# Three unmasked attentions of a decoder: scores also made with the keys on the partitions, row maxima added by TensorE

## What is computed

```python
        Q = (x @ Wq.T).reshape(B, xN, NUM_HEADS, HEAD_DIM)
        KV = (z @ Wkv.T).reshape(B, zN, 2, NUM_HEADS, HEAD_DIM)
        K = KV[:, :, 0]
        V = KV[:, :, 1]
        attn = jnp.einsum('bqhd,bkhd->bhqk', Q, K) * SCALE
        attn = jax.nn.softmax(attn, axis=-1)
        O = jnp.einsum('bhqk,bkhd->bqhd', attn, V).reshape(B, xN, DIM)
        return O @ Wo.T
```

## Time and profile before

| what | value |
|---|---|
| median of 3 runs | 4947.15 us |
| runs | 4947.15, 4937.4, 4949.03 us |
| span of the profiled execution | 4969.4 us, its own execution, 0.4% above that median |
| PE busy | 4410.3 us (89%) |
| DVE busy | 2640.3 us (53%) |
| ACT busy | 2593.2 us (52%) |
| POOL busy | 836.2 us (17%) |

### The profile page before, as it was taken

The page is one execution under the profiler, slowest core; times in us unless marked ns, Lnnn a source line. Parts: engine busy times, 40 slices in busy tenths (PEclk is TensorE's granted clock), DMA queues, the critical chain, the costliest instruction groups (busy, mean ns, idle before and its releaser), DMA issues.

```text
span 4969.4 us, 84778 instructions
## 1 busy us (share of the span) xinstructions
PE 4410.3 (89%) x29077; PEld 2535.4 (51%) x29077; DVE 2640.3 (53%) x6880; ACT 2593.2 (52%) x9813; POOL 836.2 (17%) x1454
## 2 busy tenths in 40 slices
PE   7888989989999999989799888998889888898796
PEld 3544764444454454448355444454455454554493
DVE  5555225655655655645454656556664565546523
ACT  4556434454454454453555556555655566555542
POOL 0111420011011011035021021110131021210350
PEclk9999989999999999999899989999999999999897
DMA  5000540000000000007000000000000000000172
GB/s 198 11 11 11 172 128 18 12 7 28 12 7 28 12 7 18 6 22 222 22 22 10 5 5 24 14 10 1 6 23 14 9 6 10 10 1 1 46 230 76
DMA packets 107750, 183.05 MB, mean 37 GB/s; under 512 B 13344, under 2 KB 69408, under 8 KB 107200
## 3 DMA queue, kind: packets, MB, share of 16 engines
q1 hardware_dynamic: 92544, 147.48, 9.9%
q0 software_dynamic: 13632, 28.04, 1.6%
q10 hardware_dynamic: 1152, 2.10, 0.1%
HBM read 126.33 MB, written 51.23 MB: 36 GB/s over the span
## 4 chain that ended last, share of the span: by engine, by line
PE 65%; DVE 20%; ACT 7%; issue 5%; DMA 2%; POOL 1%; SPq 0%; DVEq 0%; POOLq 0%; ACTq 0%
PE bank L713 8%; PE bank L866 7%; PE bank L883 6%; DVE rowmax L1693 6%; PE bank L745 4%; PE bank L1041 3%; PE bank L733 3%; PE bank L1152 3%; PE bank L1141 3%; PE bank L1023 3%; PE bank L790 3%; DVE probsT L1759 2%; PE bank L922 2%; PE bank L852 2%; ACT work L1323 2%
## 5 line engine op out<-in xcount | busy, mean ns | idle before, releaser
L1323 ACT ACTIVATE work<-bank,rowmax 128x128 f32<-128x128 f32 (+1 forms) x3072 | 1061.1, 398 | 208.6 <-DVE rowmax L1693 208.6
L1693 DVE TENSOR_REDUCE rowmax<-bank 128x4 f32<-128x512 f32 (+2 forms) x1152 | 614.0, 578 | 433.4 <-PE bank L866 314.8
L713 PE MATMUL bank<-mask_causal,identb 128*128 128x512 bf16 x2839 | 803.1, 394 | 22.6 <-DVE qd L1628 8.7
L883 PE MATMUL bank<-ident,work 128*128 128x128 f32 (+1 forms) x4096 | 641.0, 282 | 155.6 <-DVE probsT L1759 116.7
L1323 ACT ACTIVATION_READ_ACCUMULATOR work<-bank,rowmax 128x1 f32 x3072 | 753.1, 245 | 0.0
L883 PEld LDWEIGHTS bank<-ident,work 128*128 128x128 f32 (+1 forms) x4096 | 481.8, 144 | 377.7 <-DVE probsT L1759 196.8
L1759 DVE COPY probsT<-bank 128x512 f32<-128x512 f32 (+2 forms) x832 | 482.0, 601 | 55.3 <-PE bank L883 53.9
L713 PEld LDWEIGHTS bank<-mask_causal,identb 128*128 128x128 bf16 x2839 | 273.5, 101 | 290.7 <-issue 115.5
L866 PE MATMUL bank<-km,q 32*128 32x512 f32 (+2 forms) x1792 | 403.7, 562 | 1.9 <-issue 1.9
L2206 POOL TENSOR_TENSOR qd<-work 128x256 f32<-128x256 f32 (+1 forms) x64 | 64.7, 1012 | 1902.9 <-ACT work L1321 1836.5
L1257 ACT ACTIVATE part<-bank,eps 128x512 f32<-128x512 f32 x232 | 157.7, 680 | 383.8 <-PE bank L745 383.3
(11 more groups left out here) (336 smaller groups left out, 6902.5 us busy)
## 6 DMA issues: line engine op xcount, KB each, us to landing
slot<-in_w_L_ffn SPq DMA_DIRECT2D x78, 578.0 KB
slot<-in_w_stream SPq DMA_DIRECT2D x41, 512.0 KB
expert_rows<-slot SPq DMA_DIRECT2D x36, 516.0 KB, 6.3
slot<-in_w_L_ffn SPq DMA_DIRECT2D x39, 450.0 KB
qd<-expert_rows SPq DMA_DIRECT2D x117, 129.0 KB
back<-pair_rows SPq DMA_DIRECT2D x24, 512.0 KB, 5.3
slot<-in_w_stream SPq DMA_DIRECT2D x16, 256.0 KB
pair_rows<-qd,dest POOLq DMA_INDIRECT x234
```

The lines of the kernel that those rows point to most:

```text
L713: nc.tensor.matmul(b[:], identb[:], mask["causal"][:].unsqueeze(1).to_broadcast([P, 4, P]), start=True, stop=True)
L883: ins = nc.tensor.transpose(b[0:nk, j * P:(j + 1) * P], probs[t % 2][:, r, j, 0:nk], ident[:])
L1323: ins = nc.scalar.activation(out, raw, ACT.Exp, bias=top, accum_out=expsum[t % 2][:, 4 * r + j:4 * r + j + 1])
L1693: V.tensor_reduce(m[:, 4 * r:4 * r + J], banks.where(("scores", n, c, s, r))[:, 0:J * nk] .rearrange("p (j k) -> p j k", j=J), AX_X, ALU.m ...
```

## The change

The three attentions go through a new keyed_mha() on PE, ACT and DVE. For each item:

- PE makes the scores as before (L1026), from which only the maxima are taken, and makes them a second time with the keys on the partitions and the queries along the columns (L1037, 16 matmuls of 32 rows, 4 to a bank).
- DVE takes the 16 negated maxima, and splits each into a bf16 part and a bf16 rest in a tile `tops` (L1909, L1910). PE turns `tops` (L1045), ACT copies it to `topsT` (L1478), and PE adds it into the keyed banks by bf16 matmuls with a constant of ones and zeros, top_pick (L1056, 16 an item).
- ACT makes the exponential of a whole keyed bank in one instruction, straight to `probsT` (L1487, 4 an item). There are no transposes of probabilities and no copies of them.
- PE sums over the keys by matmuls with constant ones (L1075, 16 an item, in the attend form); ACT inverts the sums by a logarithm and an exponential (L1502, L1505). DVE's reciprocal and spread, PE's turn of the spread, ACT's copy of it and POOL's sums are gone.
- attend (L1094) and context (L1934) are as before but for the bank rings and the wait on `inverse` where it was on `wide_taken`. Output (L1106) takes its bank from the ring "second".
- The banks are two rings of three: "first" (0 to 2) for scores and turned maxima, "second" (3 to 5) for the keyed banks. Filler stands only ahead of items 0 and 1.

A round of PE is cut in two halves: scores of strips 0 and 1 of item t are interleaved with keyed matmuls of strips 2 and 3 of item t-1, and the other way round. Beside it: the constant average64 is gone (one scale in L1257's place), `after_mask` is bf16, `tops` is cleared once at the start. A part of keyed_mha() serves attentions with a mask or with a second use of the probabilities (`mask`, `post`); none of the three has these. The core of the diff:

```diff
+KEYED = ("L1_xattn", "L3_ffn", "L2_a2",)
+FRONT_ROWS, BACK_ROWS = (0, 1), (2, 3)
...
-                             "head": (4, 5)})
+                             "head": (4, 5), "first": (0, 1, 2), "second": (3, 4, 5)})
...
-            return not st["linear"] and not st["mask"] and r in POOL_SUMS
+            return not st["linear"] and not st["mask"] and not keyed(st) and r in POOL_SUMS
...
+                    if keyed(st):
+                        keyed_mha(st, second, then)
+                        return
...
+                def keyed_mha(st, second, then):
...
+                    def half(t, rows):
+                        back = BACK_ROWS if rows == FRONT_ROWS else FRONT_ROWS
+                        if t < GROUP:
+                            c, s = items[t]
...
+                            for r in rows:
+                                b = bank(("scores", n, c, s, r), ("row_max", (n, c, s, r)), "first")
...
+                        if 1 <= t <= GROUP:
+                            c, s = items[t - 1]
+                            for r in back:
+                                b = bank(("keyed", n, c, s, r), ("probsT", (n, c, s, r)), "second")
...
+                        for j in range(4):
+                            if t < GROUP:
+                                c, s = items[t]
+                                for r in rows:
+                                    g32 = slice(32 * r, 32 * r + 32)
+                                    b = banks.where(("scores", n, c, s, r))
+                                    if D == 32:
+                                        ins = nc.tensor.matmul(b[:, j * nk:(j + 1) * nk], q4[c][g32, j, s * P:(s + 1) * P],
+                                                               k4[c][g32, j, s * nk:(s + 1) * nk], start=True, stop=True)
+                                        if j == 3:
+                                            ins.then_inc(*made("scores", (n, c, s, r)))
+                                    elif j == 0:
+                                        nc.tensor.matmul(b[:, 0:4 * nk], B["q"][c][g32, s * P:(s + 1) * P],
+                                                         km[c][g32, s, :, 0:nk], start=not st["mask"], stop=True
+                                                         ).then_inc(*made("scores", (n, c, s, r)))
+                            if 1 <= t <= GROUP:
+                                c, s = items[t - 1]
+                                for r in back:
+                                    g32 = slice(32 * r, 32 * r + 32)
+                                    if D == 32:
+                                        keys, queries = k4[c][g32, j, s * nk:(s + 1) * nk], q4[c][g32, j, s * P:(s + 1) * P]
+                                    else:
+                                        keys, queries = km[c][g32, s, j, 0:nk], B["q"][c][g32, s * P:(s + 1) * P]
+                                    nc.tensor.matmul(banks.where(("keyed", n, c, s, r))[0:nk, j * P:(j + 1) * P], keys, queries,
+                                                     start=j == 0 and not st["mask"], stop=False, skip_group_check=True)
+                    def turn_tops(t):
+                        c, s = items[t]
+                        b = bank(("tops_turned", n, c, s), ("tops_taken", (n, c, s)), "first")
+                        pe.wait_ge(*have("tops", (n, c, s)))
+                        nc.tensor.matmul(b[:, 0:P], tops[:], identb[:], start=True, stop=True
+                                         ).then_inc(*made("tops_turned", (n, c, s)))
+                    def shift(t, rows):
+                        c, s = items[t]
+                        if rows == BACK_ROWS:
+                            pe.wait_ge(*have("tops_taken", (n, c, s)))
+                        for j in range(4):
+                            for r in rows:
+                                g32 = slice(32 * r, 32 * r + 32)
+                                ins = nc.tensor.matmul(banks.where(("keyed", n, c, s, r))[0:nk, j * P:(j + 1) * P],
+                                                       top_pick[g32, j:j + 1].to_broadcast([32, nk]), topsT[g32, :], start=False, stop=True,
+                                                       skip_group_check=True)
+                                if j == 3:
+                                    ins.then_inc(*made("keyed", (n, c, s, r)))
+                    def totals(t):
+                        c, s = items[t]
+                        b = bank(("summed", n, c, s), ("log_sum", (n, c, s)), "wide")
+                        for r in FRONT_ROWS + BACK_ROWS:
+                            pe.wait_ge(*have("probsT", (n, c, s, r)))
+                        for j in range(4):
+                            for r in range(4):
+                                g32 = slice(32 * r, 32 * r + 32)
+                                if D == 32:
+                                    ins = nc.tensor.matmul(b[g32, j * P:(j + 1) * P], average[0:nk, 0:32], probsT[t % 2][0:nk, r, j, :],
+                                                           start=True, stop=True)
+                                else:
+                                    ins = nc.tensor.matmul(b[g32, 0:P], W("head_ones", nk)[:, 24 - 8 * j:56 - 8 * j],
+                                                           probsT[t % 2][0:nk, r, j, :], start=j == 0, stop=j == 3)
+                        ins.then_inc(*made("summed", (n, c, s)))
...
+                    for t in range(GROUP + 2):
+                        if t == GROUP + 1:
+                            step(then)
+                        if t == 0:
+                            warm(6, "second")
+                        half(t, FRONT_ROWS)
+                        if 1 <= t <= GROUP:
+                            turn_tops(t - 1)
+                        if t >= 2:
+                            totals(t - 2)
+                        elif t == 1:
+                            warm(4, "second")
+                        if 1 <= t <= GROUP:
+                            shift(t - 1, BACK_ROWS)
+                        half(t, BACK_ROWS)
+                        if 1 <= t <= GROUP:
+                            shift(t - 1, FRONT_ROWS)
+                        for _ in range(st["hooks"].count(t)):
+                            step(second)
+                        if t == st["drained"]:
+                            drain(second)
+                        if t:
+                            step(late[0])
+                        if t >= 2:
+                            attend(t - 2)
...
+                    def take_tops(t):
+                        c, s = items[t]
+                        act.wait_ge(*have("tops_turned", (n, c, s)))
+                        nc.scalar.activation(topsT[:], banks.where(("tops_turned", n, c, s))[:, 0:P],
+                                             ACT.Copy).then_inc(*made("tops_taken", (n, c, s)))
+                    def soften(t):
+                        c, s = items[t]
+                        if t >= 2:
+                            act.wait_ge(*have("attended", (n, *items[t - 2])))
+                        for r in BACK_ROWS + FRONT_ROWS:
+                            act.wait_ge(*have("keyed", (n, c, s, r)))
+                            nc.scalar.activation(probsT[t % 2][0:nk, r, :, :], banks.where(("keyed", n, c, s, r))[0:nk, :]
+                                                 .rearrange("p (j t) -> p j t", j=4),
+                                                 ACT.Exp).then_inc(*made("probsT", (n, c, s, r)))
+                    def invert(t):
+                        c, s = items[t]
+                        w = 4 if D == 32 else 1
+                        out = spreadT[t % 2][:, 0:w, :]
...
+                        if t >= 2:
+                            act.wait_ge(*have("context", (n, *items[t - 2])))
+                        act.wait_ge(*have("summed", (n, c, s)))
+                        nc.scalar.activation(out, banks.where(("summed", n, c, s))[:, 0:w * P].rearrange("p (i t) -> p i t", i=w),
+                                             ACT.Ln, scale=float(P) if D == 32 else 1.0).then_inc(*made("log_sum", (n, c, s)))
+                        act.wait_ge(*have("log_sum", (n, c, s)))
+                        nc.scalar.activation(out, out, ACT.Exp, scale=-1.0).then_inc(*made("inverse", (n, c, s)))
...
+                    def row_max(t, rows):
+                        c, s = items[t]
+                        for r in rows:
+                            dve.wait_ge(*have("scores", (n, c, s, r)))
+                            V.tensor_reduce(rowmax[t % 2][:, 4 * r:4 * r + 4], banks.where(("scores", n, c, s, r))[:, 0:4 * nk]
+                                            .rearrange("p (j k) -> p j k", j=4), AX_X, ALU.max,
+                                            negate=True).then_inc(*made("row_max", (n, c, s, r)))
+                            if t < PER + 1 or r == BACK_ROWS[-1]:
+                                aside(t)
+                    def split_tops(t):
```

(18 more changed lines are left out.)

163 lines of the change are left out of this document (156 added, 7 removed).

## The result

The changed kernel takes 5127.7 us at the median of 4 runs (5087.0 to 5192.8), the kernel before 4948.1 (4937.4 to 4954.5). The ratio is 1.033, with a 95% interval from 1.028 to 1.038: slower by 164 us by the ratio and 180 by the medians, where 4958 was forecast and the range ended at 5000.

The account below looks back on a forecast made before the run. PE was taken to bound the kernel (89% busy, 65% of the chain). Rounds of 6.0 us plus start and end gave 4 x (5.4 - 2.3 + 0) = +12 us on the 4947.15 median: 4958, range 4915 to 5000.

Parts of the forecast that it names:

- The round: PE's distance from one item's scores to the next's in the new form: 6.0 us, 6.15 with 128 keys.
- The half: Two score blocks on two row strips beside 8 keyed matmuls on the other two: 1.05 us, 0.95 where the same form follows.
- the first rival: Scores and keyed matmuls don't run side by side in the halves: about 57 us more, so 5015; chance 0.13.
- The rule that was quoted with it: Skill's strict order of matmul starts and ends; it would make L2_a2's 1.64 us about 2.2, and the new halves unoverlapped.
- the second shifts: The bf16 shifts of a round that the next group follows at once: 0.45 us.
- The first shifts and the wait for ACT together: Shifts behind which PE waits anyway, 0.25 us, and PE's wait before the back half, 1.05 us.
- the 1.05 of the sum: PE's wait each round until ACT has exponentiated strip 2: last record 0.27, exponential 0.59, signals 0.15; 1.15 with 128 columns.
- The 0.15 for two signals: The author's own figure for two signals within PE's wait for ACT's exponential: 0.15 us.
- The stretches without a long fall: First scores to last projection: L1_xattn 59.0 us against 53.6, L2_a2 70.3 against 72.6, L3_ffn 60.9 against 60.9.
- The step that failed: Clock rival: filler goes and PE stands, costing 3.0 us in each of twelve attentions, 36 us, so 4994; chance 0.11.
- can go for nothing: The filler between PE's transposes, two L713 of 128x512, could be removed without costing time.
- POOL: Busy 17% and 1% of the chain, so the sums taken from it are worth nothing by themselves.

Follow-up runs that it names:

- later-rounds kernel: The changed kernel with three unread 128x512 bf16 matmuls in PE's pause in each round from t = 3 on, none in the opening: 5076.0 us, ratio 1.023.
- the burst: Ten wide filler matmuls in one place, instead of three, at t = 3 of the later-rounds kernel: 5018.4 us, ratio 1.013 to the kernel before.

## Why the prediction was wrong

By its own steps:

- **The round.** 6.0 us was predicted, 5.75 measured, as much in L2_a2, and in L3_ffn 5.85 (4748.65 to 4754.50). The half was 1.05 as taken: the first keyed matmuls begin 0.02 us behind the first scores. So scores and keyed matmuls run side by side, and the first rival is out. The rule that was quoted with it (the Trainium skill, TensorE: Matmul & The Clock Gate, Part 3, "The mechanism") has matmuls end in program order too; here six records of keyed matmuls end by 1844.46 and the score matmuls issued ahead of them at 1844.67, so as far as the profile's modelled ends tell, this trace doesn't agree. That the rule by itself would make 2.2 of the 1.64, as the prediction has it, doesn't follow: matmuls that end in order can still overlap. By terms, the 0.25 are mostly the second shifts, 0.32 (1848.30 to 1848.62) for 0.45. The first shifts and the wait for ACT together were 1.25 (1846.10 to 1847.35) for 1.30; PE's idle time in them, 0.83, is less than the 1.05 of the sum since that also held the last shift's own time. The 0.15 for two signals had no row; in this round they are 0.24, 0.09 from the last shift to ACT and 0.15 from ACT to PE.
- **Where PE waits.** As predicted: once a round before the back half, for ACT's probsT. There was no wait for the turned maxima; in the opening there is one of 0.66 for DVE's row maxima.
- **The stretches without a long fall.** Predicted 59.0, 70.3, 60.9; measured 57.8 to 59.2, 70.9 to 71.3, 57.8 to 60.7. ACT's busy time in L3_ffn's window is 28 us, predicted under 35. With the four long ones at 57.8 and 71, the twelve would come to 757 us against 754, and the time would have been near the 4958.
- **The step that failed** is the clock. The prediction's words were: "The first group's L3_ffn shows the price, 3.0 us of PE at a granted clock of 0.95; twelve times that is 36, so 4994", and against it "the steady rounds keep PE at work some 80%, and L3_ffn had 1.00 with PE busy for 86%". The pauses were foreseen, with their place and nearly their length; their price was read from a stretch in which the clock came back after 7 us. In the new form it can stay down for 51 to 79 us: such a fall costs 21 to 33 us, not 3, and in the profiled execution, the fastest of the four, it struck four attentions. The price of a fall is its length, and the rows of before show that for before's matmuls alone.
- **Filler "can go for nothing".** True of the kernel before, as its run without filler shows, and false of the change: 26 wide matmuls an attention, put into its pauses, take the ratio from 1.033 to 1.000.
- **POOL.** That the sums taken from it would be worth nothing was tried by no run of its own.

The cause, as far as the runs carry it: in the new form, pauses of 0.8 to 1.3 us, above all in the first rounds of an attention, let the clock fall to half (filling them takes the long falls away, with wide work and nearly as well with narrow); the old form had pauses as long and no long falls. Once it is down, rounds made mostly of matmuls of 32 rows or 32 outputs kept it down for up to 49 us in which PE never stood (the later-rounds kernel), and it came back at a stretch of matmuls over the whole array (the burst, and most projections). Open is which attention of several alike falls: the instructions are the same in all four groups, and with the pauses left in, some held their clock. How much such work it takes is open as well, and whether the width of L3_ffn's scores is what keeps its falls short.

## What to carry to other kernels

The advice rests on this one kernel. When a change takes filler or wide matmuls out of PE's stream and puts a pause in, don't price the clock by the short falls of the old stream: ask what in the new stream would bring it back, and put the whole stretch up to there at half clock into the range. The share of PE's busy time doesn't tell: 98% busy stood at half clock (later-rounds kernel), 87% at full (the kernel before without filler). Fill the pauses of the first rounds first; they were worth 0.027 of 0.033 here.

## What the runs showed that was not expected

- The same rounds with hardly a pause ran for 50 us at full clock in one kernel and at half in another; which of the two depended on what came before. The Trainium skill (TensorE: Matmul & The Clock Gate, Part 1, "What's actually happening") says that "activity releases the throttle"; 53.3 busy us of 54.6 did not release it here, so for this work the trace doesn't agree.
- At half clock a round went from 5.75 to 9.72 us, 1.7 times, since ACT's share of it stays as it is.
- Two forms of unequal length on different strips, 308 columns beside 128, take the 1.05 us of 16 equal ones.
- Three wide filler matmuls in a pause of 0.83 us cost nothing: in L1_xattn the first chain's projection begins 39.3 us after the first scores with them and without. The whole stretch is 55.5 us with them and 57.8 without, where the last 6 us are at half clock.
